# A two-stage attention model on one core: the first stage's Newton passes recompute their differences on TensorE

## The chip, the core and the metric

The kernel runs on one core of one Trainium2 chip. The metric is the device time of one execution in microseconds (us): the median of the kernel before is 6143.65 us over three runs (6131.52 to 6153.98).

## What is computed

Eight sequences of 512 tokens and 128 features go through one attention layer with a root-finding normalisation instead of a softmax, and then through six layers of windowed attention with a gated feed-forward block. Only the first layer, with the layer norms around it, is touched by the change:

```python
s = jnp.einsum('bhnd,bhmd->bhnm', Q, K) * scale            # 16 heads of 8 features
lam = jnp.where(mask, s, -1e30).max(-1) + 1.0              # causal mask
for _ in range(4):
    d = jnp.maximum(lam[..., None] - s, EPS)
    f = jnp.where(mask, 1 / d, 0.0).sum(-1) - 1.0
    fp = -jnp.where(mask, 1 / d ** 2, 0.0).sum(-1)
    lam = lam - f / fp
p = jnp.where(mask, 1 / jnp.maximum(lam[..., None] - s, EPS), 0.0)
return jnp.einsum('bhnm,bhmd->bhnd', p / p.sum(-1, keepdims=True), V)
```

So each head needs one row maximum, four Newton passes with two row sums each, and a final pass whose weights are multiplied with the values.

## The kernel before

Three stages run one after another: `stage1` (the first attention layer), `stage2` (the six layers) and `stage3` (a last transpose and sum). Each engine has its own written-out program, and semaphores order them.

In `stage1` the work is tiled as sequence, then quad (four heads; four quads), then head, then block of 128 query tokens. Because of the causal mask, query block u of a head needs 128·(u+1) keys, so a head has four units of 128, 256, 384 and 512 columns, 1280 columns in all, with the 128 queries on the partitions. The loop over sequences (`Fori(0, BATCH)`) holds four quads N, and while quad N is iterated, the scores of quad N+1 are made and the weights of quad N-1 are applied to the values.

- TensorE: `scores` (L212) multiplies 8 rows of queries with 8 rows of keys for each unit, once per quad, and adds the causal mask with an identity matmul (L214). The four heads of a quad sit on partitions 0, 32, 64 and 96, so each score matmul uses one group of 32 rows. `turn` (L225) transposes the finished weights, `weigh` (L238) multiplies them with the values (20 records for a head), `project` (L205) makes queries and keys.
- VectorE: `scores_in` (L489) copies scores into `S` with a running maximum; `newton` squares the root for even heads (L506, with the sum of 1/d) and squares again (L517, with the sum of 1/d²), then three tiny operations (L523, L525, L528) update `lam`.
- ScalarE: L386 makes 1/sqrt(lam - s) for each unit with `lam` as its bias, in five passes; L394 squares the odd heads; L358 copies transposed weights out of PSUM; L336 and L340 copy projections.
- GpSimd: L447 squares the final root into the weights `W`.

A matmul on fp32 data appears in the trace as two records, each with its own weight load. The lines at which the order is set on ScalarE are these:

```python
for t in range(ITERS + 1):
    for pair in (0, 1):
        if t:
            act.wait_ge(s_lam, N * 2 * ITERS + 2 * (t - 1) + pair + 1)
...
                nc.scalar.activation(R[:, h, c], S[:, par, h, c], ACT.Abs_reciprocal_sqrt,
                                     bias=lam[:, par, i:i + 1], scale=-1.0).then_inc(s_root, 1)
```

Of the kernel before, what the change touches and what calls it, by code (L numbers as in the profile page):

```python
# [18 lines left out]
P = 128  # L19
# [3 lines left out]
MASKED1 = -1e28  # L23
# [8 lines left out]
OFF = [sum(UNIT[:u]) for u in range(NBLK)]  # L32
# [3 lines left out]

ACT_SQ = [(t, h) for t in range(ITERS) for pair in (0, 1) for h in (2 * pair, 2 * pair + 1)
          if h % 2 == 1]
DVE_SQ = [(t, h) for t in range(ITERS) for pair in (0, 1) for h in (2 * pair, 2 * pair + 1)
          if (t, h) not in ACT_SQ]  # L40

PIECES = [(0, 3), (OFF[2], 3), (OFF[3], 4)]
BLOCKS = [[(0, 0), (1, 0), (1, 1)], [(2, k) for k in range(3)], [(3, k) for k in range(4)]]
NPC = len(PIECES)

# [16 lines left out]
NCONST = C_RO + 4 * SEQ  # L62


def stage1(nc, x, consts, w1qk, w1vo, x1d, hist):
    with ExitStack() as ctx:
# [10 lines left out]
        cmask = sb("cmask", [P, P])  # L77
        identb = sb("identb", [P, P], BF16)
        cmaskb = sb("cmaskb", [P, P], BF16)
# [12 lines left out]
        S = sb("S", [P, 2, QUAD, ROW])  # L92
        R = sb("R", [P, QUAD, ROW])
        W = sb("W", [P, QUAD, ROW])
        WT = sb("WT", [P, 2, SEQ])
# [3 lines left out]
        smax = sb("smax", [P, 2, NU])  # L99
        lam = sb("lam", [P, 2, NU])  # L100
        sum1 = sb("sum1", [P, NU])
        sum2 = sb("sum2", [P, NU])
        step = sb("step", [P, 2, NU])
        stat = [sb(f"stat{i}", [P, NBLK, 6]) for i in range(2)]
# [4 lines left out]
        psS = ps("psS", [P, NBLK, SEQ])  # L109
        psT = ps("psT", [P, 2, SEQ])  # L110
# [10 lines left out]
        s_score = sem("s_score")  # L121
        s_evac = sem("s_evac")
        s_lam0 = sem("s_lam0")
        s_root = sem("s_root")
        s_asq = sem("s_asq")
        s_dsq = sem("s_dsq")
        s_sq2 = sem("s_sq2")
        s_step = sem("s_step")
        s_lam = sem("s_lam")
        s_w = sem("s_w")  # L130
        s_tr = sem("s_tr")
        s_trev = sem("s_trev")
        s_pv = sem("s_pv")
        s_quad = sem("s_quad")
# [6 lines left out]
        s_rs = [sem("s_rs_in"), sem("s_rs_out")]  # L141

        M_PRO, M_B = 9, 13
        E_PRO, E_B = 9, 12
# [3 lines left out]

        @block.sync
        def _(sp):  # L150
            sp.dma_start(ident[:, :], consts[:, C_ID:C_ID + P]).then_inc(const_in, 16)
            sp.dma_start(cmask[:, :], consts[:, C_CM:C_CM + P]).then_inc(const_in, 16)
            sp.dma_start(wqk[:, :, :, :], w1qk).then_inc(const_in, 16)
            sp.dma_start(wvo[:, :, :], w1vo).then_inc(const_in, 16)
            sp.dma_start(xin[:, :, :], x[0].rearrange("(k p) d -> p k d", p=P)).then_inc(xin_in, 16)

            def tokens(t, i):
                return t[bass.ds(i, 1)].rearrange("a (k p) d -> p (a k) d", p=P)

            def store(b):  # L160
                sp.wait_ge(s_x1, b + 1)
                sp.dma_start(tokens(x1d, b - 1), x1[:, :, :]).then_inc(x1_out, 16)
                sp.wait_ge(s_mev, b * E_B + E_PRO + 2)
                sp.dma_start(hist[bass.ds(b - 1, 1)].rearrange("a p n -> (a p) n"), houtT[:, :])\
                  .then_inc(hist_out, 16)

            def sequence(b, last=False):
                first = isinstance(b, int) and b == 0
                if not first:
                    sp.wait_ge(s_x1, b)  # L170
                    sp.dma_start(xres[:, :, :], tokens(x, b - 1)).then_inc(xres_in, 16)
                sp.wait_ge(s_ln[0], b * LN + LN)
                if last:
                    sp.sem_inc(xin_in, 16)
                else:
                    sp.dma_start(xin[:, :, :], tokens(x, b + 1)).then_inc(xin_in, 16)
                if not first:
                    store(b)

            sequence(0)  # L180
            with sp.Fori(1, BATCH - 1) as b:
                sequence(b)
            sequence(BATCH - 1, last=True)
            sp.wait_ge(s_x1, BATCH)
            sp.dma_start(xres[:, :, :], tokens(x, BATCH - 1)).then_inc(xres_in, 16)
            store(BATCH)

            sp.wait_ge(x1_out, 16 * BATCH + 32)
            sp.wait_ge(hist_out, 16 * BATCH + 32)

        @block.tensor
        def _(pe):
            def m_free(n_ev):
                pe.wait_ge(s_mev, n_ev)

            def turn_h(base):
                pe.wait_ge(s_ln[0], base[1])
                m_free(base[0])
# [7 lines left out]

            def scores(N, j, h):


                for u in range(NBLK):  # L210
                    pe.wait_ge(s_evac, N * NU + h * NBLK + u + 1)
                    pe.matmul(psS[:, u, 0:UNIT[u]], qT[32 * h:32 * h + DH1, j, u * P:(u + 1) * P],  # L212
                              kT[32 * h:32 * h + DH1, j, 0:UNIT[u]], start=True, stop=True)
                    pe.matmul(psS[:, u, u * P:UNIT[u]], identb[:, :], cmaskb[:, :],  # L214
                              start=False, stop=True, skip_group_check=True).then_inc(s_score, 1)

            def turn(N, h, i):

                t = N * QUAD * NPC + h * NPC + i
                if i == 0:  # L220
                    pe.wait_ge(s_w, N * QUAD + h + 1)
                pe.wait_ge(s_trev, t + 1)
                c, n = PIECES[i]
                for m in range(n):
                    mm = pe.transpose(psT[:, (h * NPC + i) % 2, m * P:(m + 1) * P],  # L225
                                      W[:, h, c + m * P:c + (m + 1) * P], ident[:, :])
                mm.then_inc(s_tr, 1)

            def weigh(N, jprev, h, i):

                t = N * QUAD * NPC + h * NPC + i
                pe.wait_ge(s_trev, t + 3)
                if h == 0 and i == 0:
                    pe.wait_ge(s_attn, N + 1)
                for m, (u, k) in enumerate(BLOCKS[i]):
                    head = jprev * QUAD + h
                    o = (u * QUAD + h) * VW
                    mm = pe.matmul(psO[:, o:o + VW], WT[:, (h * NPC + i) % 2, m * P:(m + 1) * P],  # L238
                                   vals[:, k, head, :], start=(k == 0), stop=(k == u))
                mm.then_inc(s_pv, 1)  # L240

            def head_out(N, jprev, h):
                for i in range(NPC):
                    turn(N, h, i)
                    if i:
                        weigh(N, jprev, h, i - 1)
                weigh(N, jprev, h, NPC - 1)

            def turn_attn(b):
                pe.wait_ge(s_attn, b * NQ + 2)  # L250
                m_free(b * E_B + E_PRO)
# [4 lines left out]
            def out_project(b):  # L256
                m_free(b * E_B + E_PRO + 1)
# [5 lines left out]
            def turn_out(b):  # L263
                pe.wait_ge(s_ln[1], b * LN + LN)
                for k in range(NBLK):
# [3 lines left out]
            def values(b):  # L269
                m_free(b * E_B + E_PRO + 2)  # L270
                for k in range(NBLK):
                    mm = pe.matmul(psM[:, k * P:(k + 1) * P], hT[:, k * P:(k + 1) * P], wvo[:, 0, :],
                                   start=True, stop=True)
                mm.then_inc(s_m, 1)

            pe.wait_ge(const_in, 64)
# [6 lines left out]
            for j in range(NQ):  # L283
                project(0, j, 1 + 2 * j)
                project(1, j, 2 + 2 * j)
            pe.wait_ge(s_mev, E_PRO)
            for h in range(QUAD):
                scores(0, 0, h)

            with pe.Fori(0, BATCH) as b:  # L290
                for j in range(NQ):
                    N = b * NQ + j
                    nxt, prev = (j + 1) % NQ, (j - 1) % NQ
                    e = b * E_B + E_PRO
                    scores(N + 1, nxt, 0)
                    if j == 1:
                        pe.wait_ge(s_mev, e + 3)
                    head_out(N, prev, 0)
                    head_out(N, prev, 1)
                    scores(N + 1, nxt, 1)  # L300
                    head_out(N, prev, 2)
                    head_out(N, prev, 3)
                    scores(N + 1, nxt, 2)
                    if j == 0:
                        turn_attn(b)
# [1439 lines left out]
```

## Time and profile before

| what | value |
|---|---|
| median of three runs | 6143.65 us (6131.52 to 6153.98) |
| profiled execution, time / span | 6155.39 us / 6153.6 us |
| `stage1`: last store issued at (us from the span's start) | 2689.42 us |
| `stage2`: first DMA issued at / first matmul at | 2691.90 / 2705.69 us |
| one sequence in `stage1`, from the repetition of the trace | 327 us |

The profile is that of one execution. "Busy" is the time in which an engine executed at least one instruction; PEld is TensorE's loading of weights, which can overlap its matmuls. [...]

### The profile page before, as it was taken

To read this page: it belongs to the slowest core of one execution; us is meant where nothing else is said; L and a number is where in the kernel's file an instruction comes from. 1 tells how busy PE (TensorE), PEld (TensorE's weight loads), DVE (VectorE), ACT (ScalarE), POOL (GpSimd) and SP (SyncE) were. 2 spreads that over 40 slices of the span, in tenths; PEclk is the share of its full clock that TensorE was granted. 3 is DMA by queue.
4 is the path that set the end of the run, shared out by engine and by line. 5 is a ranking of instruction groups with operands and counts; after the bars stand their busy time and mean duration, and the time that the engine had idled before them with its cause. 6 is when DMAs were issued, how large, how long until landed. Compare 5 with 4: busy or idle time off the path is not lost. (4 is left out here: it accounts for less than half of the span.)

```text
span 6153.6 us, 167056 instructions
## 1 busy us (share of the span) xinstructions
PE 5086.1 (83%) x61548; PEld 2941.8 (48%) x61548; DVE 4768.3 (77%) x11291; ACT 3546.7 (58%) x6859; POOL 2569.4 (42%) x1151
## 2 busy tenths in 40 slices
PE   6777767676767776769999998999899999989996
PEld 3444444444444444435555554555455545545553
DVE  5777777777777777848888887888788888878884
ACT  4777776777767776745545554455454545444552
POOL 1101011111101011136666676667666667666672
PEclk9999999999999999999999999999999999999997
DMA  0000000000000000024445444444444444444443
GB/s 11 3 3 6 1 8 1 6 3 6 3 6 3 6 0 6 1 67 103 103 109 122 108 101 105 109 115 106 108 105 103 116 114 104 100 106 115 110 108 84
DMA packets 231561, 383.60 MB, mean 62 GB/s; under 512 B 35712, under 2 KB 60928, under 8 KB 230656
## 3 DMA queue, kind: packets, MB, share of 16 engines
q1 hardware_dynamic: 226560, 370.71, 25.6%
q8 instruction: 540, 8.85, 0.6%
q10 hardware_dynamic: 4224, 2.10, 0.1%
q14 instruction: 237, 1.94, 0.1%
HBM read 51.81 MB, written 18.87 MB: 11 GB/s over the span
## 5 line engine op out<-in xcount | busy, mean ns | idle before, releaser
L386 ACT ACTIVATE R<-S,lam 128x128 f32<-128x128 f32 (+3 forms) x2560 | 1191.1, 551 | 200.6 <-DVE lam L528 158.3
L447 POOL TENSOR_TENSOR W<-R 128x1280 f32<-128x1280 f32 x128 | 309.9, 2441 | 2335.6 <-ACT R L386 2335.6
L212 PE MATMUL psS<-kT,qT 8*128 8x128 f32 (+3 forms) x1056 | 755.3, 816 | 311.5 <-DVE S L489 222.2
L517 DVE CUSTOM_DVE_ANT_0 R<-R 128x128 f32<-128x128 f32 (+3 forms) x2048 | 987.1, 536 | 14.1
L1300 POOL TENSOR_TENSOR m<-m 128x1024 f32<-128x1024 f32 x384 | 902.5, 2361 | 69.7 <-DVE m L1408 69.4
L506 DVE CUSTOM_DVE_ANT_0 R<-R 128x128 f32<-128x128 f32 (+3 forms) x1024 | 503.3, 523 | 495.5 <-ACT R L386 471.3
L917 PE MATMUL pb<-xs,wg 128*128 128x512 f32 x1536 | 763.4, 632 | 49.8 <-DMA xs<-hist 36.5
L238 PE MATMUL psO<-vals,WT 128*128 128x9 f32 x2640 | 587.0, 356 | 160.8 <-ACT WT L358 160.8
L238 PEld LDWEIGHTS psO<-vals,WT 128*128 128x128 f32 x2640 | 589.4, 331 | 209.5 <-ACT WT L358 209.5
L1431 DVE SCALAR_TENSOR_TENSOR nf<-rn,m 128x1024 f32<-128x1024 f32 x384 | 617.0, 1638 | 87.5 <-ACT rn L1162 74.7
L1153 ACT ACTIVATE lnn<-pb,cst 128x1024 f32<-128x1024 f32 x192 | 213.9, 1114 | 803.0 <-PE pb L924 803.0
L1148 ACT ACTIVATE sq<-pb 128x1024 f32<-128x1024 f32 x384 | 382.0, 1021 | 490.7 <-PE pb L917 490.7
L1306 POOL TENSOR_TENSOR sm<-sm,mx 128x1024 f32<-128x1024 f32 x192 | 451.7, 2352 | 503.9 <-DVE mx L1422 503.8
L1296 POOL TENSOR_TENSOR sqs<-sq 128x1024 f32<-128x1024 f32 x192 | 457.0, 2380 | 225.6 <-ACT sq L1148 225.6
L1311 POOL TENSOR_TENSOR pr<-pr,rsum 128x1024 f32<-128x1024 f32 x192 | 410.8, 2140 | 289.1 <-DVE rsum L1444 285.2
L1407 DVE TENSOR_TENSOR m<-pb,tab 128x1024 f32<-128x1024 f32 x384 | 464.7, 1210 | 15.1 <-ACT sq L1148 12.1
L1408 DVE TENSOR_TENSOR m<-pb,tab 128x1024 f32<-128x1024 f32 x384 | 465.6, 1212 | 0.0
L394 ACT ACTIVATE R<-R 128x128 f32<-128x128 f32 (+3 forms) x1024 | 464.5, 458 | 0.0
L917 PEld LDWEIGHTS pb<-xs,wg 128*128 128x128 f32 x1536 | 291.1, 200 | 361.2 <-issue 354.0
L358 ACT COPY WT<-psT 128x384 f32<-128x384 f32 (+1 forms) x396 | 194.6, 509 | 461.9 <-PE psT L225 461.9
L212 PEld LDWEIGHTS psS<-kT,qT 8*128 8x128 f32 x1056 | 262.4, 307 | 407.7 <-DVE S L489 243.3
L924 PE MATMUL pb<-sqs,ones 128*128 128x512 f32 x768 | 392.5, 635 | 29.6 <-DVE m L1408 22.6
(112 smaller groups left out, 8709.3 us busy)
## 6 DMA issues: line engine op xcount, KB each, us to landing
qkn<-nf SPq DMA_DIRECT2D x1536, 128.0 KB
vr<-v SPq DMA_DIRECT2D x96, 768.0 KB, 6.0
vr<-v SPq DMA_DIRECT2D x96, 192.0 KB, 5.6
xr<-hist SPq DMA_DIRECT2D x48, 256.0 KB, 2.9
hist<-xo SPq DMA_DIRECT2D x48, 256.0 KB, 4.1
wg<-wqkv SPq DMA_DIRECT2D x24, 384.0 KB, 3.6
xs<-hist SPq DMA_DIRECT2D x48, 128.0 KB
vr<-v SPq DMA_DIRECT2D x96, 64.0 KB, 6.2
```

The costliest lines, as they stand in the source:

```text
L212: pe.matmul(psS[:, u, 0:UNIT[u]], qT[32 * h:32 * h + DH1, j, u * P:(u + 1) * P], kT[32 * h:32 * h + DH1, j, 0:UNIT[u]], start=True, stop=True)
L238: mm = pe.matmul(psO[:, o:o + VW], WT[:, (h * NPC + i) % 2, m * P:(m + 1) * P], vals[:, k, head, :], start=(k == 0), stop=(k == u))
L386: nc.scalar.activation(R[:, h, c], S[:, par, h, c], ACT.Abs_reciprocal_sqrt, bias=lam[:, par, i:i + 1], scale=-1.0).then_inc(s_root, 1)
L394: nc.scalar.activation(R[:, h, c], R[:, h, c], ACT.Square, accum_out=sum1[:, i:i + 1]).then_inc(s_asq, 1)
L506: nc.vector.tensor_tensor_reduce(out=R[:, h, c], in0=R[:, h, c], in1=R[:, h, c], scale=1.0, scalar=0.0, op0=ALU.mult, op1=ALU.add, accum_o ...
L517: nc.vector.tensor_tensor_reduce(out=R[:, h, c], in0=R[:, h, c], in1=R[:, h, c], scale=1.0, scalar=0.0, op0=ALU.mult, op1=ALU.add, accum_o ...
L917: mm = pe.matmul(out[:, half, :], wg[:, g, c:c + P], xs[:, 0:SEQ], start=True, stop=True)
L1296: nc.gpsimd.tensor_tensor(sqs[:, :, :], sq[:, :, 0, :], sq[:, :, 1, :], ALU.add).then_inc(s_sqs, 1)
L1300: nc.gpsimd.tensor_tensor(m1[:, which, :, :], m1[:, which, :, :], m2[:, which, ::-1, :], ALU.add)\
L1407: nc.vector.tensor_tensor(m1[:, which, :, :], src[:, :, :], tab[:, which, 0, :, :], ALU.mult)
L1408: nc.vector.tensor_tensor(m2[:, which, :, :], src[:, :, :], tab[:, which, 1, :, :], ALU.mult)\
L1431: nc.vector.scalar_tensor_tensor(out=nf[:, which, :, :], in0=rn[:, which, :].unsqueeze(1).broadcast_to([P, 2, SEQ]), scalar=1e12, in1=m1[: ...
```

## The change

`stage1` is rewritten; `stage2` and `stage3` stay. What is different:

- **Nine rows.** `lam` is put as a ninth row under the eight query rows, and a row of ones (`C_KR`) under the keys, whose evacuation multiplies by -SCALE1. So one matmul gives lam - s, and it is repeated for every pass: one pass for the minimum (p = 0), four Newton passes, one final pass (p = 5). `S` and the evacuation of scores go.
- **Pairs of heads.** `differences` issues the matmuls of two heads alternately, each head into its own three PSUM banks `psD[i]`, and then six bf16 mask matmuls. There is no second buffer: head i of the next pair waits until ScalarE has read head i of this one (`free`).
- **Whole heads.** ScalarE does one root of 128x1280 straight from PSUM and one square of 128x1280 for each head. VectorE takes the sums with four `bn_stats` of the square, from whose counts, means and variances eight small operations (`small`) make the new `lam`, for a whole quad.
- **lam's way back.** `lam` is transposed on VectorE and four DMAs put it into the ninth rows of `qT`.
- **The final pass** is made with keys and queries exchanged, so that the weights come out transposed; the transposes and their copies go.
- **Four quads in flight.** A table of 24 slots for each sequence, `SLOTS`, gives each slot one quad and pass: quad j does pass p in slot (5j + 4p) mod 24. Between two passes of one quad lie three other slots.

```diff
+NSLOT = 24
+LAST = ITERS + 1
+SLOTS = {}
+for _j in range(NQ):
+    for _p in range(LAST + 1):
+        SLOTS[(5 * _j + 4 * _p) % NSLOT] = (_j, _p, (5 * _j + 4 * _p) // NSLOT)
...
+            def send_lam(b, s):
+                j = SLOTS[s][0]
+                sp.wait_ge(s_lam, rank(b, s, UPDATE) + 1)
+                sp.sem_inc(held["sp"], 1)
+                for q in range(4):
+                    sp.dma_start(qT[DH1:P:32, j, :].rearrange("h (u q p) -> h u q p", u=NBLK, q=4)[:, :, q, :],
+                                 lamT[32 * q:32 * q + NU, j, :]).then_inc(lam_in[j], 16)
...
+                    if SLOTS[t[1]][1] == 0:
+                        pe.wait_ge(s_min, QUAD * rank(*t, FIRST) + h + 1)
+                    elif SLOTS[t[1]][1] == LAST:
+                        pe.wait_ge(s_rootf, QUAD * rank(*t, FINAL) + h + 1)
+                    else:
+                        pe.wait_ge(s_root, QUAD * rank(*t, NEWTON) + h + 1)
+                    pe.sem_inc(held["pe"], 1)
+
+                if p < LAST:
+                    for u in UORD:
+                        for i, h in enumerate(heads):
+                            if u == UORD[0]:
+                                free(i)
+                            r = slice(32 * h, 32 * h + KROW)
+                            pe.matmul(psD[i][:, UOFF[u]:UOFF[u] + UNIT[u]], qT[r, j, u * P:(u + 1) * P], kT[r, j, 0:UNIT[u]],
+                                      start=(u != UORD[2]), stop=True, skip_group_check=True)
...
+                for i, h in enumerate(heads):
+                    for c, n in spans:
+                        mm = pe.matmul(psD[i][:, c:c + n * P], identb[:, :],
+                                       cmaskb[:, int(p == LAST), 0:n, :].rearrange("p a n -> p (a n)"),
+                                       start=False, stop=True, skip_group_check=True)
+                    mm.then_inc(s_d, 1)
...
+                    act.wait_ge(s_d, QUAD * rank(b, s, range(LAST + 1)) + h + 1)
+                    nc.scalar.activation(dst, psD[i][:, 0:ROW], ACT.Abs_reciprocal_sqrt, bias=zero[:, 0:1])\
+                        .then_inc(s_rootf if p == LAST else s_root, 1)
...
+                    act.wait_ge(s_root, QUAD * rank(b, s, NEWTON) + h + 1)
+                    nc.scalar.activation(W[:, h, :], W[:, h, :], ACT.Square).then_inc(s_w, 1)
...
+                ins = nc.vector.bn_stats(out=stats[:, s % 2, i, :], in_=W[:, h, UOFF[u]:UOFF[u] + UNIT[u]])
```

On TensorE, at the head of the loop over sequences, the program before has one head's four units, each followed by its mask, once for a quad (`psS` are the scores in PSUM, `cmaskb` and `identb` mask and identity in bf16):

```order
L212 MATMUL psS<-kT,qT 128x128
L214 MATMUL psS<-cmaskb,identb 128x128
L211 REGISTER_ALU
L212 MATMUL psS<-kT,qT 128x256
L214 MATMUL psS<-cmaskb,identb 128x128
L211 REGISTER_ALU
L212 MATMUL psS<-kT,qT 128x384
L214 MATMUL psS<-cmaskb,identb 128x128
L211 REGISTER_ALU
L212 MATMUL psS<-kT,qT 128x512
L214 MATMUL psS<-cmaskb,identb 128x128
```

At the same place the changed program has this for a pair of heads (`x2` are the two heads; the two rows of 128x512 at the start stand apart, because each waits for its own bank):

```order
L298 ISA
L307 MATMUL psD<-kT,qT 128x512
L298 REGISTER_ALU
L307 MATMUL psD<-kT,qT 128x512
L307 MATMUL psD<-kT,qT 128x384 x2
L307 MATMUL psD<-kT,qT 128x128 x2
L307 MATMUL psD<-kT,qT 128x256 x2
L321 MATMUL psD<-cmaskb,identb 128x128
L321 MATMUL psD<-cmaskb,identb 128x256
L321 MATMUL psD<-cmaskb,identb 128x128 x2
L321 MATMUL psD<-cmaskb,identb 128x256
L321 MATMUL psD<-cmaskb,identb 128x128
```

Such a block now stands 48 times in the loop's body for each sequence, twice in each of 24 slots, where the scores of 16 single heads stood before.

On ScalarE, inside a pass, the program before works unit by unit (`R` is the root, `S` the scores in SBUF):

```order
L386 ACTIVATE R<-S,lam 128x128
L386 ACTIVATE R<-S,lam 128x256
L386 ACTIVATE R<-S,lam 128x384
L386 ACTIVATE R<-S,lam 128x512
L393 ISA
L394 ACTIVATE R,sum<-R 128x128
L393 REGISTER_ALU
L394 ACTIVATE R,sum<-R 128x256
```

The changed program has, for a pair of heads in a Newton slot, two roots out of PSUM and two squares, and then what else the slot holds:

```order
L469 ACTIVATE W<-psD,zero 128x1280
L465 REGISTER_ALU
L468 REGISTER_ALU
L469 ACTIVATE W<-psD,zero 128x1280
L479 ACTIVATE W<-W 128x1280 x2
L431 REGISTER_ALU
L432 COPY qT<-psM 128x512
```

Eight roots for two heads have become two, and they read the PSUM banks that TensorE has to fill again next.

## Rows read from the trace of the kernel before

**Rows 1.** The page: span, busy time of each engine.

```profile
span 6153.6 us, 167056 instructions
PE 5086.1 (83%) x61548; PEld 2941.8 (48%) x61548; DVE 4768.3 (77%) x11291; ACT 3546.7 (58%) x6859; POOL 2569.4 (42%) x1151
```

**Rows 2.** Busy time by stretch: a sequence of stage1, pieces of stage2.

```profile
core 0: us, PE busy (x) PEld busy (x) DVE busy (x) ACT busy (x) POOL busy (x), PEclk, DMA share, GB/s
350.00:677.00 327.00, 229.79 (x719) 146.70 (x718) 247.63 (x1046) 234.75 (x643) 38.74 (x16) 1.00 0.01 4
...
2731.68:2732.11 0.43, 0.43 (x33) 0.43 (x33) 0.00 (x0) 0.32 (x1) 0.43 (x1) 0.50 0.00 0
...
3300.00:6000.00 2700.00, 2546.06 (x44739) 1382.76 (x44737) 2237.07 (x2312) 1351.15 (x1398) 1815.49 (x814) 0.98 0.47 109
```

**Rows 3.** Waits between 350 and 677 us: us in total, times, longest.

```profile
DVE R L506 <- ACT R L386: 63.3, 17, 7.9
...
ACT R L386 <- DVE lam L528: 19.8, 4, 6.1
```

**Rows 4.** Timeline of TensorE, one head's scores in the prologue.

```profile
42.07 0.79 PE L212 MATMUL psS<-kT,qT 8*128 8x128 f32 x2
42.79 0.29 PE L214 MATMUL psS<-cmaskb,identb 128*128 128x128 bf16 x1
43.01 1.22 PE L212 MATMUL psS<-kT,qT 8*128 8x256 f32 x2
...
44.37 1.64 PE L212 MATMUL psS<-kT,qT 8*128 8x384 f32 x2
...
46.17 2.07 PE L212 MATMUL psS<-kT,qT 8*128 8x512 f32 x2
...
48.39 0.79 PE L212 MATMUL psS<-kT,qT 8*128 8x128 f32 x2
```

**Rows 5.** Timeline of TensorE where stage2 begins.

```profile
2705.69 5.92 PE L917 MATMUL pb<-xs,wg 128*128 128x512 f32 x8 [16.98 <-DMA xs<-hist]
2711.45 1.88 PE L989 MATMUL pb<-wg,xs 128*128 128x512 f32 x4
```

**Rows 6.** Timeline of TensorE: matmuls on eight tiles of 64 rows by 32 columns.

```profile
2728.00 3.75 PE L924 MATMUL pb<-sqs,ones 128*128 128x512 f32 x4 [2.94 <-POOL sqs L1296]
2731.68 2.06 PE L940 MATMUL pb<-qkn 64*32 64x64 f32 x128
```

**Rows 7.** Timeline of TensorE in stage1: values.

```profile
404.25 3.00 PE L238 MATMUL psO<-vals,WT 128*128 128x9 f32 x14
```

**Rows 8.** Groups by form, 340 to 667 us: busy us, mean ns of one.

```profile
L386 ACT ACTIVATE R<-S,lam 128x512 f32<-128x512 f32 x81 | 57.5, 710 | 0.0
L386 ACT ACTIVATE R<-S,lam 128x384 f32<-128x384 f32 x82 | 49.4, 603 | 0.0
L447 POOL TENSOR_TENSOR W<-R 128x1280 f32<-128x1280 f32 x16 | 38.7, 2442 | 285.8 <-ACT R L386 285.8
L205 PE MATMUL psM<-hT,wqk 128*128 128x512 f32 x16 | 16.4, 1130 | 13.2 <-ACT qT L336 11.2 <-ACT kT L336 2.0
L489 DVE TENSOR_SCALAR_CACHE_REDUCE S<-psS 128x512 f32<-128x512 f32 x16 | 11.0, 685 | 0.0
L525 DVE SCALAR_TENSOR_TENSOR step<-sum,step 128x8 f32<-128x8 f32 x32 | 7.5, 233 | 1.1
L489 DVE TENSOR_SCALAR_CACHE_REDUCE S<-psS 128x128 f32<-128x128 f32 x16 | 4.6, 290 | 0.0
L455 DVE BATCH_NORM_STATS2 stat<-x 128x6 f32<-128x128 f32 x4 | 0.9, 280 | 0.0
```

**Rows 9.** The page's groups: a square of 128x1024 out of PSUM.

```profile
L1148 ACT ACTIVATE sq<-pb 128x1024 f32<-128x1024 f32 x384 | 382.0, 1021 | 490.7 <-PE pb L917 490.7
```

**Rows 10.** DMA issues up to 2700 us: median us to landing.

```profile
x1d<-x SPq DMA_DIRECT2D x8, 256.0 KB, 2.3
```

**Rows 11.** Timeline of SyncE where stage1 ends.

```profile
2689.42 0.34 SPq L164 DMA_DIRECT2D hist<-houtT  x1
```

More of the change, by code:

```diff
@@ L35 @@
 VW = DH1 + 1
[L37 to L44, printed above, removed]
 DEPTH, H2, DH2, WIN = 6, 16, 64, 32
@@ L62 @@
 NCONST = C_RO + 4 * SEQ
+C_CT = NCONST
+C_KR = C_CT + P
+C_HC = C_KR + 1
+NCOLS = C_HC + 2 * NU
+UORD = (3, 2, 0, 1)
+UOFF = {u: sum(UNIT[w] for w in UORD[:i]) for i, u in enumerate(UORD)}
+KORD = (0, 3, 1, 2)
+KLEN = [SEQ - k * P for k in range(NBLK)]
+KOFF = {k: sum(KLEN[w] for w in KORD[:i]) for i, k in enumerate(KORD)}
+BANKS1 = 3
+KROW = DH1 + 1
+NSLOT = 24
[4 more added lines that the diff above has]
+        SLOTS[(5 * _j + 4 * _p) % NSLOT] = (_j, _p, (5 * _j + 4 * _p) // NSLOT)
 def stage1(nc, x, consts, w1qk, w1vo, x1d, hist):
@@ L107, in stage1 @@
         zero = sb("zero", [P, 1])
-        psS = ps("psS", [P, NBLK, SEQ])
-        psT = ps("psT", [P, 2, SEQ])
+        psD = [ps(f"psD{i}", [P, BANKS1 * SEQ]) for i in range(2)]
         psO = ps("psO", [P, SEQ])
@@ new lines, in rank, with fits, junk @@
+        def rank(b, s, passes, quad=None):
+            def fits(t):
+                return SLOTS[t][1] in passes and (quad is None or SLOTS[t][0] == quad)
+            if isinstance(b, int) and b == 0:
+                return sum(fits(t) for t in range(NSLOT) if t < s or not live(b, t))
+            return b * sum(fits(t) for t in range(NSLOT)) + sum(fits(t) for t in range(s) if live(b, t))
+        def junk(passes, quad=None):
+            return sum(SLOTS[t][1] in passes and (quad is None or SLOTS[t][0] == quad) for t in range(NSLOT) if SLOTS[t][2])
@@ L161, in store, with store_x1 @@
+            def store_x1(b):
                 sp.wait_ge(s_x1, b + 1)
+                sp.sem_inc(held["sp"], 1)
                 sp.dma_start(tokens(x1d, b - 1), x1[:, :, :]).then_inc(x1_out, 16)
[L163 to L167, printed above, removed]
-                first = isinstance(b, int) and b == 0
[L169 to L178, printed above, removed]
@@ L180, in _, with store_h @@
-            sequence(0)
-            with sp.Fori(1, BATCH - 1) as b:
[L182 to L186, printed above, removed]
+            def store_h(b, n_ev):
+                sp.wait_ge(s_mev, n_ev)
+                sp.sem_inc(held["sp"], 1)
+                sp.dma_start(hist[bass.ds(b - 1, 1)].rearrange("a p n -> (a p) n"), houtT[:, :]).then_inc(hist_out, 16)
@@ new lines, in body @@
+            def body(b):
+                first = isinstance(b, int) and b == 0
+                tail = isinstance(b, int) and b == BATCH
+                for s in range(NSLOT):
+                    if s == 0 and not first:
+                        sp.wait_ge(s_x1, b)
+                        sp.sem_inc(held["sp"], 1)
+                        sp.dma_start(xres[:, :, :], tokens(x, b - 1)).then_inc(xres_in, 16)
+                    if s == 1 and not tail:
+                        sp.wait_ge(s_ln[0], b * LN + LN)
+                        sp.sem_inc(held["sp"], 1)
+                        if isinstance(b, int) and b == BATCH - 1:
+                            sp.sem_inc(xin_in, 16)
+                        else:
+                            sp.dma_start(xin[:, :, :], tokens(x, b + 1)).then_inc(xin_in, 16)
+                    if s == 20 and not first:
+                        store_x1(b)
+                    if s == 23 and not first:
+                        store_h(b, b * E_B + E_PRO + (2 if tail else 9))
+                    t = prev(b, s)
+                    if live(b, s) and t is not None and SLOTS[t[1]][1] < LAST:
+                        send_lam(*t)
@@ L194, in m_free, with project, turn_h @@
                 pe.wait_ge(s_mev, n_ev)
-            def turn_h(base):
-                pe.wait_ge(s_ln[0], base[1])
-                m_free(base[0])
+                pe.sem_inc(held["pe"], 1)
+            def project(which, j, n_ev):
+                m_free(n_ev)
+                pe.matmul(psM[:, :], wqk[:, which, j, :], hT[:, :], start=True, stop=True).then_inc(s_m, 1)
+            def turn_h(n_ev, n_ln):
+                pe.wait_ge(s_ln[0], n_ln)
+                pe.sem_inc(held["pe"], 1)
+                m_free(n_ev)
                 for k in range(NBLK):
@@ L201, in turn_h @@
                 mm.then_inc(s_m, 1)
-            def project(which, j, n_ev):
-                m_free(n_ev)
-                pe.matmul(psM[:, :], wqk[:, which, j, :], hT[:, :], start=True, stop=True).then_inc(s_m, 1)
[L207 to L240, printed above, removed]
@@ new lines, in weigh @@
+            def weigh(b, s, h):
+                j = SLOTS[s][0]
+                r = rank(b, s, FINAL)
+                if h == 0:
+                    pe.wait_ge(s_attn, r + 1)
+                    pe.sem_inc(held["pe"], 1)
+                pe.wait_ge(s_wf, QUAD * r + h + 1)
+                pe.sem_inc(held["pe"], 1)
+                for u in range(NBLK):
+                    o = (u * QUAD + h) * VW
+                    for k in range(u + 1):
+                        c = KOFF[k] + (u - k) * P
+                        mm = pe.matmul(psO[:, o:o + VW], WF[:, h, c:c + P], vals[:, k, j * QUAD + h, :],
+                                       start=(k == 0), stop=(k == u))
+                mm.then_inc(s_pv, 1)
@@ L252, in turn_attn, with values @@
+            def values(n_ev):
+                m_free(n_ev)
+                for k in range(NBLK):
+                    mm = pe.matmul(psM[:, k * P:(k + 1) * P], hT[:, k * P:(k + 1) * P], wvo[:, 0, :], start=True, stop=True)
+                mm.then_inc(s_m, 1)
+            def turn_attn(b, n_ev):
+                pe.wait_ge(s_attn, rank(b, 12, FINAL) + 1)
+                pe.sem_inc(held["pe"], 1)
+                m_free(n_ev)
                 for k in range(NBLK):
@@ L267, in turn_out, with body @@
                 mm.then_inc(s_m, 1)
[L269 to L276, printed above, removed]
+            def body(b):
+                e = b * E_B + E_PRO
+                tail = isinstance(b, int) and b == BATCH
+                first = isinstance(b, int) and b == 0
+                for s in range(NSLOT):
+                    for pair in range(2):
+                        if live(b, s):
+                            differences(b, s, pair)
+                        for f in (1, 6, 11, 20):
+                            if s == f + 1 + pair and live(b, f):
+                                weigh(b, f, 2 * pair)
+                                weigh(b, f, 2 * pair + 1)
+                        if not tail:
+                            if (s, pair) == (2, 0):
+                                project(0, 1, e)
+                            if (s, pair) == (2, 1):
+                                project(1, 1, e + 1)
+                            if (s, pair) == (7, 0):
+                                project(0, 2, e + 2)
+                            if (s, pair) == (7, 1):
+                                project(1, 2, e + 3)
+                            if (s, pair) == (12, 0):
+                                project(0, 3, e + 4)
+                            if (s, pair) == (12, 1):
+                                project(1, 3, e + 5)
+                            if (s, pair) == (14, 0):
+                                values(e + 6)
+                        if (s, pair) == (15, 1):
+                            turn_attn(b, e + (0 if tail else 7))
+                        if (s, pair) == (16, 1):
+                            out_project(e + (1 if tail else 8))
+                        if (s, pair) == (20, 0):
+                            turn_out(b)
+                        if not tail:
+                            if (s, pair) == (21, 0):
+                                turn_h(e + 9, b * LN + 2 * LN)
+                            if (s, pair) == (22, 0):
+                                project(0, 0, e + 10)
+                            if (s, pair) == (22, 1):
+                                project(1, 0, e + 11)
@@ L419, in _ @@
-            for h in range(QUAD):
-                pieces(BATCH * NQ, h)
-            m = BATCH * M_B + M_PRO
-            evac(attnT[:, :], m + 1)
-            rstd(1, BATCH * LN + 3)
-            evac_out(BATCH)
+            evac(qT[:, 0, :], 2)
+            evac_keys(0, 3)
+            body(0)
+            with act.Fori(1, BATCH) as b:
+                body(b)
+            body(BATCH)
         @block.gpsimd
         def _(pool):
-            nc.gpsimd.memset(W[:, :, :], 1.0)
             nc.gpsimd.memset(vals[:, :, :, :], 1.0)
@@ L553, in _ @@
+            ins.then_inc(masks, 1)
             dve.wait_ge(masks, 2)
```

503 lines of the change are left out of this document (273 added, 230 removed).

## Prediction

> **What bounds the kernel now.** I read the page first [rows 1]: no engine is near 100% over the span, but the span is an average over two long stages. The busy time by stretch parts them [rows 2]: one sequence of `stage1` takes 327 us, in which VectorE is busy for 247.6, ScalarE for 234.8, TensorE for 229.8 and GpSimd for 38.7. Eight of these are 2616 us of the 2689 us at which the last store of the stage is issued [rows 11]; `stage2` isn't touched. The waits [rows 3] show what holds `stage1`: VectorE waits 63.3 us for ScalarE's root and ScalarE 19.8 us for VectorE's `lam`. They form one loop, root, square, sum, `lam`, and neither can run ahead. TensorE has about 100 us to spare in each sequence. The change takes work off this loop and puts it on TensorE, so the question is what a pair of heads costs there.
>
> **TensorE's clock in stage1.** The printed clock is no help here, because the first record of it comes later. The durations tell. A record of a projection, 128x512 on all 128 rows, takes 1130 ns [rows 8]; at the start of `stage2` four records of the same size take 1.88 us together, 0.43 us apart, where the eight before them took 5.92 [rows 5]. [...] In the prologue the four heads' scores follow one another as densely as they can (6.32 us for a head, from 42.07 to 48.39, the next starting at once), and the last still costs what the first did [rows 4]. Score matmuls on 8 rows don't raise the clock, even without a gap.
>
> **The new cycle.** A pair of heads now goes through a loop that has no second buffer: TensorE fills two sets of banks, ScalarE reads them, TensorE fills them again. [...]
>
> - *Score stream of one head.* From 384 to 512 columns the duration grows from 1.64 to 2.07 us, 0.43 us for 128 columns, so 1280 columns stream in 4.3 us; each matmul has 0.36 us beside that (0.79 - 0.43) [rows 4]. Nine rows instead of eight use the same group of 32 and cost the same.
> - *Do the two heads overlap?* The trace has no pair of such matmuls, but it has others: 128 records on eight tiles, two row groups by four column groups, take 2.06 us [rows 6], at a granted clock of 0.50 [rows 2]. At that clock 128 columns stream in 0.43 us over two records, so a record of 64 columns takes 0.107, and 128 of them in a line 13.7 us. They ran 6.6 deep; column groups alone give at most four, so both row groups worked at once. I take full overlap: the pair streams in 4.3 us, counted from the later head.
> - *Masks.* One mask takes 0.21 us from its start to the next instruction (42.79 to 43.01) [rows 4]. The pair has six, with eight blocks of 128 columns: between 0.8 us (half of 0.21 for each block, if the weight load hides) and 1.7; I take 1.3, of which head A's end comes 0.4 earlier.
> - *Roots.* A unit of 512 takes 710 ns and one of 384 takes 603, so 0.84 ns for a column [rows 8]; 1280 columns give 1.35 us. A square of 1024 columns from PSUM takes 1021 ns [rows 9], by which 1280 would be 1.24. I take 1.3 for a root and 1.25 for a square.
>
> Count from the moment at which head A's masks have landed: root A until 1.3, root B until 2.6, with 0.1 for the semaphore head B's stream runs from 2.7 to 7.0 (head A's, begun 1.3 earlier, is hidden behind it), and head A's masks land 0.85 later: **7.85 us for a pair**. The squares (2 x 1.25) run meanwhile. Bounds: with roots of 1.24 and masks of 0.8 in all, 7.45; with the 0.36 of four matmuls unhidden, 9.3.
>
> **The sum for one sequence.** 24 slots of two pairs, 48 x 7.85 = 377 us (in the four slots of the first pass VectorE's minimum of 1280 columns, (685-290)/384 = 1.03 ns for a column [rows 8], stands in for the root, 1.4 us and some small operations between: +4). The values: 14 records take 3.00 us [rows 7], 0.214 each; 20 records for a head, 40 for a pair, are 8.6 us, of which the next pair's wait for root A hides 1.3: 8 pairs x 7.3 = 58. The projections (two records of about 1 us [rows 8]), the output projection and the transposes each lie in the same gap and stick out by about 0.7 us: +10. Together **449 us against 327**, +122, and eight times that +976. At the ends: the first sequence has no other quad to fill slots 1 to 3, the last one's chain of passes runs nearly alone, and there is a tail as before; about +15 in all. That is +991 on the profiled 6155, so 7146, and as the median lies 12 us below that execution, **7135 us**.
>
> **What is hidden, and by what.** ScalarE has 80 roots and 64 squares, 184 us, and some 7 for copies: 191 of 449. VectorE: `bn_stats` of 128 columns takes 0.22 us from one to the next (0.9 us for four) [rows 8], so a head takes 4 x 0.22 + 768 x 1.03 ns = 1.7 us, 64 heads 107 us; 16 minima 22; 20 updates of eight operations at 0.23 [rows 8], 37; norms some 13: 179. GpSimd stays at 38.7. `lam`'s way back is about 2 us of small operations, four issues and a landing of about 2.3 us [rows 10], against three slots of 15.7 us before it is needed. SyncE's queue has it behind the stores of `x1` and `hist`, whose data are ready slots earlier. If that cover went, the stall would be TensorE's, at the first matmul of a slot, with everything queued behind.
>
> [...]
>
> **The rivals.**
>
> 1. *The clock rises in stage1: faster.* TensorE's activity grows (two row groups at once, masks on 128 rows, a projection right behind them). [...] For: `stage2` holds the high clock over 2700 us [rows 2]. Against: rows 4, and that TensorE must stop for each root. [...] Chance 0.14.
> 2. *The row groups don't overlap: slower still.* Each record waits for the one before, as within one head in rows 4. Head B's stream then starts when A's ends: 1.4 + 8.6 = 10.0 instead of 7.0, +3.0 us, and 384 x 3.0 = 1150: **about 8290 us**. For: every fp32 matmul is two records with weight loads on the same group, issued head by head. Against: rows 6. With partial overlap it lies between. Chance 0.12.
> 3. *The change doesn't bind on TensorE at all* but on another term that I hide (the small operations, the DMA of `lam`, code loading): each slot would then be longer by a few us without a busier engine, 7300 to 8000 us. Chance 0.05. That the time stays within 0.3% needs a cycle of 6.1 us by accident; 0.01.
>
> The forecast has 0.68. Its own range follows from 7.45 and 9.3 us: 384 x (-0.4) and 384 x 1.45 give 6980 to 7690. With the second and third rival the range is **6900 to 8300**, which leaves out the faster case and the extremes. A measurement of this kernel tells about 0.3% from no change: faster 0.15, same 0.02, slower 0.83.
>
> **What the changed kernel's profile would show.** Right: a sequence of about 450 us; L307 records of 128x512 at about 1.06 us or longer, two heads' records overlapping in time; TensorE idle some 1.4 us before each pair, released by ScalarE's root; ScalarE busy for about 40% of `stage1`, VectorE too; almost no wait for `lam`. Wrong: L307 records of 128x512 near 0.6 us (rival 1); a pair's masks 10 us after its first matmul (rival 2); waits for the DMA of `lam` (rival 3).

## The result, and the profile after

| | time | against before |
|---|---|---|
| before, runs beside it | 6148.81 us (6131.52 to 6169.75, 4 runs) | |
| changed kernel | 7011.18 us (6984.98 to 7029.06, 4 runs) | ratio 1.1397 [1.1346, 1.1449] |

The change costs 862 us; 986 (7135 - 6149) were forecast. The page of the changed kernel, beside [rows 1], has the span, the engines' busy time and the granted clock in 40 slices:

```profile
span 6983.2 us, 169488 instructions
PE 6343.6 (91%) x67000; PEld 3832.7 (55%) x67000; DVE 4023.9 (58%) x6681; ACT 3143.1 (45%) x3001; POOL 2545.1 (36%) x1151
...
PE   7899998989989899898969999989989998998996
...
PEclk6555555555555555555579999999999999999998
```

Against the kernel before VectorE lost 744 us of work and ScalarE 404, and TensorE gained 1258. The clock line now has records for `stage1`, where [rows 2] prints 1.00 for a stretch without one: 0.5 for most of it. Here the low clock is the 0.50 of such lines and the high clock their 1.00. Two stretches, with the columns of [rows 2]:

```profile
1000.00:1500.00 500.00, 453.12 (x1647) 302.40 (x1646) 183.43 (x562) 209.49 (x183) 36.76 (x16) 0.52 0.01 3
...
4000.00:6900.00 2900.00, 2723.40 (x48316) 1482.81 (x48315) 2401.34 (x2496) 1448.67 (x1498) 1945.31 (x874) 0.98 0.47 109
```

In `stage1` TensorE is busy for 91% of the time, VectorE for 37% and ScalarE for 42%; `stage2` looks as before. The waits between 1000 and 2000 us, beside [rows 3] (who waits, for whom, us in total, times, longest):

```profile
DVE stats L605 <- ACT W L479: 569.9, 76, 22.9
ACT W L469 <- PE psD L321: 292.3, 69, 9.1
...
PE psD L307 <- ACT W L469: 46.7, 42, 1.3
...
PE psD L307 <- DVE part L598: 22.7, 21, 3.6
```

VectorE waits for ScalarE's squares, ScalarE for TensorE's masks, and TensorE for nothing but ScalarE's (or, in the first pass, VectorE's) reading of the banks, 1.1 us on average. No wait for `lam`'s DMA is on the list. So the loop without a second buffer should be what bounds `stage1`; the experiments below test it. The timeline shows two turns of it:

```profile
1010.66 2.02 PE L265 MATMUL psM<-hT,wqk 128*128 128x512 f32 x2
...
1012.61 3.01 PE L307 MATMUL psD<-kT,qT 9*128 9x512 f32 x16
...
1015.55 0.61 PE L321 MATMUL psD<-cmaskb,identb 128*128 128x128 bf16 x6
...
1017.45 5.82 PE L307 MATMUL psD<-kT,qT 9*128 9x512 f32 x16 [1.29 <-ACT W L469]
...
1023.21 1.03 PE L321 MATMUL psD<-cmaskb,identb 128*128 128x128 bf16 x6
1023.85 2.55 ACT L469 ACTIVATE W<-psD,zero 128x1280 f32<-128x1280 f32 x2 [3.01 <-PE psD L321]
1023.89 2.23 SPq L212 DMA_DIRECT2D qT<-lamT  x4
...
1024.03 8.65 PE L338 MATMUL psO<-vals,WF 128*128 128x9 f32 x40
```

The pair at 1017.45 is the usual one: 16 records for both heads in 5.82 us, where one head took 6.32 with its masks in [rows 4]. The pair at 1012.61 ran mostly at the high clock, right behind masks and a projection: 3.01 us. Its true counterpart is not the usual pair but the pair at the same place one sequence earlier. That one stands behind a projection too, has no wait for a root in its stream, and ran at the low clock (the last three rows are stretches around the pair at 1012.61, with the columns of [rows 2]; the clock stands before the last two numbers):

```profile
570.78 5.16 PE L307 MATMUL psD<-kT,qT 9*128 9x512 f32 x16
575.87 1.03 PE L321 MATMUL psD<-cmaskb,identb 128*128 128x128 bf16 x6
...
1010.50:1013.20 2.70, 2.70 (x7) 1.11 (x5) 0.00 (x0) 2.70 (x3) 0.00 (x0) 0.50 0.00 0
1013.30:1016.60 3.30, 2.86 (x22) 2.04 (x20) 2.39 (x6) 3.23 (x4) 0.00 (x0) 1.00 0.00 0
1016.80:1023.00 6.20, 5.55 (x16) 3.66 (x16) 3.94 (x16) 4.04 (x4) 0.00 (x0) 0.50 0.01 3
```

So the high clock makes 3.0 us of 5.2. There were 23 such spells in the whole of `stage1`, together 79 us of 3556. The queue issues the four DMAs of `lam` within 2.23 us; the profile gives no time at which they land. Groups by form, 1000 to 1440 us:

```profile
L307 PE MATMUL psD<-kT,qT 9*128 9x512 f32 x160 | 117.7, 1094 | 33.0 <-ACT W L469 18.8 <-DVE part L598 9.8 <-ACT WF L469 4.3
...
L469 ACT ACTIVATE W<-psD,zero 128x1280 f32<-128x1280 f32 x64 | 81.5, 1323 | 124.5 <-PE psD L321 124.2
L479 ACT ACTIVATE W<-W 128x1280 f32<-128x1280 f32 x64 | 77.6, 1266 | 0.0
...
L598 DVE TENSOR_REDUCE part<-psD 128x10 f32<-128x1280 f32 x16 | 23.4, 1486 | 21.1 <-PE psD L321 18.4 <-issue 2.8
```

### The profile page after: what moved, and what is told of

It is laid out like the page before. It is cut to its first block and busy times, and to the rows that moved or that the text cites. A ratio compares the mean times of both kernels' runs of the same rounds, so it can differ in the third digit from the quotient of the medians.

```text
span 6983.2 us, 169488 instructions
## 1 busy us (share of the span) xinstructions
PE 6343.6 (91%) x67000; PEld 3832.7 (55%) x67000; DVE 4023.9 (58%) x6681; ACT 3143.1 (45%) x3001; POOL 2545.1 (36%) x1151
## 5 line engine op out<-in xcount | busy, mean ns | idle before, releaser
L605 DVE BATCH_NORM_STATS2 stats<-W 128x6 f32<-128x512 f32 (+3 forms) x2048 | 882.1, 480 | 2011.6 <-ACT W L479 2011.6
L307 PE MATMUL psD<-kT,qT 9*128 9x128 f32 (+3 forms) x5120 | 1734.7, 734 | 267.2 <-ACT W L469 151.2
L307 PEld LDWEIGHTS psD<-kT,qT 9*128 9x128 f32 x5120 | 1047.9, 313 | 907.9 <-issue 883.9
L552 POOL TENSOR_TENSOR WF<-WF 128x1280 f32<-128x1280 f32 x128 | 294.1, 2319 | 3219.9 <-ACT WF L469 3219.9
L469 ACT ACTIVATE W<-psD,zero 128x1280 f32<-128x1280 f32 x512 | 651.7, 1323 | 1013.7 <-PE psD L321 1011.9
L479 ACT ACTIVATE W<-W 128x1280 f32<-128x1280 f32 x512 | 620.7, 1266 | 0.0
L338 PEld LDWEIGHTS psO<-vals,WF 128*128 128x128 f32 x2560 | 550.2, 331 | 3.5
L338 PE MATMUL psO<-vals,WF 128*128 128x9 f32 x2560 | 550.1, 360 | 0.0
L469 ACT ACTIVATE WF<-psD,zero 128x1280 f32<-128x1280 f32 x128 | 163.0, 1324 | 657.7 <-PE psD L321 657.7
L316 PE MATMUL psD<-qT,kT 9*128 9x512 f32 (+3 forms) x1024 | 374.0, 752 | 70.0 <-ACT WF L469 27.8
```

Of the source, the lines that this page charges most:

```text
L307: pe.matmul(psD[i][:, UOFF[u]:UOFF[u] + UNIT[u]], qT[r, j, u * P:(u + 1) * P], kT[r, j, 0:UNIT[u]], start=(u != UORD[2]), stop=True, skip_ ...
L338: mm = pe.matmul(psO[:, o:o + VW], WF[:, h, c:c + P], vals[:, k, j * QUAD + h, :], start=(k == 0), stop=(k == u))
L469: nc.scalar.activation(dst, psD[i][:, 0:ROW], ACT.Abs_reciprocal_sqrt, bias=zero[:, 0:1])\
L479: nc.scalar.activation(W[:, h, :], W[:, h, :], ACT.Square).then_inc(s_w, 1)
L605: ins = nc.vector.bn_stats(out=stats[:, s % 2, i, :], in_=W[:, h, UOFF[u]:UOFF[u] + UNIT[u]])
```

## The experiments

My theory: TensorE's stream at the low clock and the wait for the roots follow one another in a loop; two heads overlap almost fully. The rivals: no overlap, a clock that could be raised, or a bound elsewhere.

### The two heads one after the other

```diff
-                    for u in UORD:
-                        for i, h in enumerate(heads):
+                    for i, h in enumerate(heads):
+                        for u in UORD:
```

(and the same for `KORD` in the final pass)

> The changed kernel, but differences issues all four matmuls of head A and then all four of head B instead of alternating; same work, same masks, same waits. My theory (the two row groups stream at once, and this hides one head's 4.3 us in each cycle of 7.87): without alternation head B's stream starts when head A's ends, the cycle grows by about 3 us to 10.9, a sequence by 48 x 3 = 145 us, and the time is about 7011 + 1150 = 8160 us. Rival (the overlap comes from the queue, whatever the order of issue, or the cycle is bound elsewhere): the cycle stays near 7.9 and the time within 100 us of 7011.

Measured: 7766.78 us (one run, as are the next four), between the 8160 of the theory and the 7011 of its rival. Its timeline of TensorE:

```profile
1029.43 7.75 PE L307 MATMUL psD<-kT,qT 9*128 9x512 f32 x16 [1.08 <-ACT W L469]
1037.11 1.03 PE L321 MATMUL psD<-cmaskb,identb 128*128 128x128 bf16 x6
1039.23 7.75 PE L307 MATMUL psD<-kT,qT 9*128 9x512 f32 x16 [1.08 <-ACT W L469]
```

The pair's stream grows from 5.82 to 7.75 us and the cycle, from one pair's first record to the next one's, from 7.87 to 9.80 (1029.43 to 1039.23): the alternation is worth 1.93 us for each pair, so the heads do overlap in the changed kernel, and rival 2 is out. But without any overlap head B would start 4.40 us behind head A (one head's stream, below) instead of 1.22, so 3.2 us were to be expected, and I had expected about 3. The records say why it is less. In a window of 20 ns, 1032.54 to 1032.56, three of them are at work (count, shortest/median/longest duration in ns, first and last start, forms):

```profile
L307 PE MATMUL psD<-kT,qT x3: 416/842/1217, 1031.9 to 1032.5; 9*128 9x384 f32 x1, 9*128 9x128 f32 x1, 9*128 9x512 f32 x1
```

Head A's order is 512, 384, 128, 256 columns, two records each. Head B's first record of 512 is at work here while only one of A's last four has started, though the program issues it behind all of them. Head B overtakes: it starts 3.12 us behind head A, 1.27 of the two streams still overlap, and that was missing from my forecast.

### All 32 rows of a group

```diff
-                            r = slice(32 * h, 32 * h + KROW)
+                            r = slice(32 * h, 32 * h + 32)
```

> The changed kernel with 32 rows in each difference matmul instead of 9; rows 9 to 31 of queries and keys are zeros, so the results are the same. Theory (a matmul costs by its columns, and the row group is taken whole): records of 128x512 keep their 1.06 us between starts, the cycle stays 7.87, and the time is 7011 within 30 us. [...]

Measured: 6990.99 us, within the changed kernel's range. The median cycle is 7.87 us again, and the granted clock in 1000 to 3000 us stays near 0.5:

```profile
1000.00:3000.00 2000.00, 1806.46 (x6517) 1194.19 (x6517) 714.60 (x2177) 847.51 (x733) 165.46 (x72) 0.52 0.01 4
```

The time at the high clock in `stage1` is 154 us instead of 79, but the granted clock of the whole execution, 0.752, lies within the 0.734 to 0.755 of the changed kernel's four runs. Nine rows or 32 cost the same, as I had taken for eight and nine, and with 32 the clock of `stage1` is as low as with nine.

### Filler matmuls on 128 rows

```diff
+                    for n in range(FILL * (i == 0)):
+                        pe.matmul(psD[1][:, ROW:ROW + 2 * P], identb[:, :], cmaskb[:, 0, :, :].rearrange("p a n -> p (a n)"),
+                                  start=False, stop=True, skip_group_check=True)
```

They stand behind head A's masks, where head A's root runs beside them, and write columns that nobody reads. Four:

> The changed kernel with four more bf16 matmuls of 128 rows by 256 columns in each pair, between head A's masks and head B's, into the unused end of head B's banks. [...] Theory (the slow clock is what makes the new first stage slow, and what lifts it is full-height activity): the printed clock in the first stage rises well above 0.51, pairs at 5.7 to 6.1 us appear in number, and the time falls below 6800. Rival (this much doesn't lift the clock): the clock stays near 0.51 and the time near 7011, up to 7150 if the four are not hidden.

Eight:

> [...] If the clock stays slow, they stick out by about 0.8 us less what root A hides: cycle 7.9 to 8.7, time 7011 to 7320. If the clock rises for good, the cycle is 5.7 to 6.2 us and the sequence 48 x 6 + 30 = 320 us, and the time is near 6100, the kernel before.

Measured: 7088.79 us with four, 7073.73 with eight. Four give 85 us at the high clock in `stage1`, hardly more than the 79 without them, so what was called the rival came true. Eight give 597 us in 167 spells, which is neither of the two cases that I had named. The clock of the window and a turn of the loop with eight:

```profile
1000.00:2000.00 1000.00, 972.70 (x4113) 636.05 (x4114) 365.84 (x1091) 430.70 (x364) 78.18 (x34) 0.60 0.01 3
...
1030.86 1.91 PE L327 MATMUL psD<-cmaskb,identb 128*128 128x256 bf16 x8
...
1033.13 3.97 PE L308 MATMUL psD<-kT,qT 9*128 9x512 f32 x16
```

The pair's stream takes 3.97 us here, partly at the high clock, and the fillers 1.9. The cycles (from masks to masks) fall mainly into two groups, 8.8 us at the low clock and 6.6 with a spell in them. Against the 7.87 without fillers the first lose 0.9 (the 0.8 of the forecast was my estimate) and the second gain 1.3, and the total comes out 63 us longer. So eight fillers raised the clock in part, to 0.60 in this window, but not for a profit.

### Half a root

```diff
-                    nc.scalar.activation(dst, psD[i][:, 0:ROW], ...)
+                    nc.scalar.activation(dst[:, 0:ROW // 2], psD[i][:, 0:ROW // 2], ...)
```

(`W` and `WF` are filled with ones once, at the start.) This kernel leaves out the root of half the columns, so it tells about time only.

> The changed kernel with the root taken of only the first 640 of 1280 columns; the other half of W and WF keeps its initial ones, so the Newton sums are not the reference's. Theory (the pair's cycle is root A, root B, head B's stream and the masks, one after another, because the banks have no second set): a root takes about 0.8 us instead of 1.33, two of them are 1.1 us shorter from start to start, and the cycle falls from 7.87 to about 6.8; 40 of 48 pairs have a root, so 8 x 40 x 1.1 = 350 us less, 6660 us. Rival (TensorE itself is full, it only looks as if it waited): the cycle falls by less than 0.3 and the time by less than 100 us.

Measured: 6798.74 us. The root takes 790 ns instead of 1323, and two turns are

```profile
1035.92 5.29 PE L307 MATMUL psD<-kT,qT 9*128 9x512 f32 x16 [0.55 <-ACT W L469]
1041.14 1.03 PE L321 MATMUL psD<-cmaskb,identb 128*128 128x128 bf16 x6
1042.72 5.29 PE L307 MATMUL psD<-kT,qT 9*128 9x512 f32 x16 [0.55 <-ACT W L469]
```

6.80 us apart. Both roots are on the path: 1.07 us less of them takes 1.07 off the ordinary cycle, although only 0.53 of it shows as a shorter idle time (from 1.08 to 0.55). The other half is in the stream, which shrinks from 5.82 to 5.29, because head B's first record no longer waits as long behind head A's. The total lies above the 6660 forecast, for two reasons. A sequence takes 409.5 us, 27.5 less than the changed kernel's, where 40 times 1.1 was expected. Of its 48 pairs, 8 wait for minima instead of roots and 8 have 8.65 us of values over the roots, and neither give anything; 6 have a projection there and give 0.5 each; 26 give 1.07. That makes 31 us, of which the rarer high clock (48 us of `stage1` instead of 79) takes back some 3. And what follows the first matmul of `stage2` took 3459.7 us instead of 3427.4 in this execution.

### bf16 rows in three parts

Queries and keys in bf16, each as a near part and a remainder: a group of 32 rows holds three products of eight rows and `lam` in two rows, 26 in all. A bf16 matmul is one record instead of two, and in the changed kernel at the low clock a bf16 mask record of 256 columns is followed by the next 0.21 us later, an fp32 record of 256 columns 0.43 us later. VectorE makes the remainder as the projection is read, `lam` goes through eight DMAs, and the scale moves into the root.

```diff
-        qT = sb("qT", [P, NQ, SEQ])
-        kT = sb("kT", [P, NQ, SEQ])
+        qT = sb("qT", [P, NQ, SEQ], BF16)
+        kT = sb("kT", [P, NQ, SEQ], BF16)
...
+                nc.vector.scalar_tensor_tensor(out=(qT, kT)[which][:, j, :], in0=near[:, :], scalar=fixed[:, 1 + which:2 + which],
+                                               in1=psM[:, :], op0=ALU.mult, op1=ALU.add).then_inc(s_mev, 1)
...
+                nc.vector.tensor_tensor(lamb[:, j, 1, 0:NU], l, lamb[:, j, 0, 0:NU], ALU.subtract).then_inc(s_far, 1)
```

> [...] 40 pairs at 4.9 and 8 first ones at 5, values 8 x 7, others 10: about 305 us for a sequence against 324.5 in the kernel before, 8 x 305 + 45 + 3450 = 5935 us. Rival (the loop over TensorE and ScalarE has other costs that the stream covers, such as lam's DMAs or weight loads): the cycle stays above 6 us and the time above 6400.

Measured: 5928.02 us (5923.32 to 5931.36, 4 runs), ratio to before 0.9634 [0.9613, 0.9656]. The clock did not change (0.52 between 1000 and 2000 us), the stream did. Its timeline:

```profile
1047.88 1.22 PE L314 MATMUL psD<-kT,qT 26*128 26x512 bf16 x7 [0.82 <-DVE part L615]
...
1049.04 1.03 PE L328 MATMUL psD<-cmaskb,identb 128*128 128x128 bf16 x6
1049.68 2.55 ACT L480 ACTIVATE W<-psD,zero 128x1280 f32<-128x1280 f32 x2 [2.97 <-PE psD L328]
...
1052.12 2.43 ACT L490 ACTIVATE W<-W 128x1280 f32<-128x1280 f32 x2
...
1052.37 1.22 PE L314 MATMUL psD<-kT,qT 26*128 26x512 bf16 x7 [0.64 <-ACT W L480]
...
1053.53 1.03 PE L328 MATMUL psD<-cmaskb,identb 128*128 128x128 bf16 x6
...
1054.44 2.54 ACT L480 ACTIVATE W<-psD,zero 128x1280 f32<-128x1280 f32 x2
```

The masks stand 4.49 us apart (1049.04 to 1053.53) instead of 7.87. Roots and squares now fill ScalarE without a gap in this stretch, 4.76 us from root to root, which is also the median cycle (the 4.9 of the forecast was my estimate): in the pairs without values the bound has moved there. In the stage as a whole ScalarE is busy for 612 of 1000 us, and the pairs behind which the values stand take 10.6 to 12.5 us, in which ScalarE waits for TensorE. A sequence takes 301 us, under the 324.5 of before. With all else of the change in place, and a little work added on VectorE and the queue, a shorter stream turns 14% slower into 3.6% faster.

### The values over four slots

```diff
-                            if s == f + 1 + pair and live(b, f):
-                                weigh(b, f, 2 * pair)
-                                weigh(b, f, 2 * pair + 1)
+                            if s in (f + 1, f + 2) and live(b, f):
+                                weigh(b, f, 2 * (s - f - 1) + pair)
```

One head's 20 records now follow each pair, so that each block can hide behind a root, instead of 40 behind every other pair. On the changed kernel:

> The changed kernel with one head's product with the values behind each of four pairs, instead of two heads' behind each of two pairs of the same two slots. Theory (of each such block the next pair's wait for root A hides about 1.4 us, and the rest is on the path): four blocks hide 5.6 us where two hid 2.8, 4 x 2.8 = 11 us for a sequence, so the time falls by about 90 us to 6920. Rival (what sticks out isn't on the path, because ScalarE catches up later): no difference within 20 us.

Measured: 6964.81 us (6954.18 to 6979.29, 4 runs), ratio to before 1.1319 [1.1287, 1.1352]; the interval of the change itself begins at 1.1346. The two overlap, so the ratios alone don't show a gain, though all four times lie under the changed kernel's lowest, 6984.98. The trace shows it: a sequence takes 432 us, 5 less, where 11 were expected. The high clock fell from 23 spells to 3 (79 us to 10); 20 spells of 2.2 us are 5.5 us for a sequence, which is the half that is missing. On the bf16 rows:

> The two last edits together. With a cycle bound by ScalarE at 4.9 us, TensorE has a little time of its own in each cycle, so a block of 4.3 us sticks out by some 2.5 us instead of 7.2 for a double one: 16 x 2.5 = 40 against 57 us; about 288 us for a sequence and 5800 us. If the values aren't on the path any more, both edits together cost the same as the bf16 rows alone.

Measured: 5836.52 us (5826.56 to 5846.93, 4 runs), ratio to before 0.9494 [0.9471, 0.9516]. One sequence is 287 us, of which ScalarE works 182 and TensorE 210:

```profile
1800.00:2087.00 287.00, 209.94 (x1036) 134.73 (x1036) 174.33 (x518) 182.20 (x158) 36.59 (x16) 0.51 0.02 4
```

This is the fastest version, 5% under the kernel before; 288 us for a sequence and 5800 us were expected.

## Why the prediction held, point by point

- **What bounds.** Right. The path was to be root A, root B, head B's stream, head A's masks. Counted from the moment at which head A's masks have landed, the trace has head A's first record at 1.48 us, head B's at 2.70, the next masks at 7.23 and A's masks landed at 7.87. The forecast had 2.7, 7.0 and 7.85. The median of 384 cycles is 7.87 us. Two errors cancel in it: head B's stream and what follows it took 4.53 instead of 4.3, head A's masks 0.64 instead of 0.85. The test with half a root shows that both roots belong to the path, that with bf16 rows that the stream does.
- **Overlap.** Right, and shown by the records of the pair and by the heads in turn: taking the alternation away adds 1.93 us. Head B's stream, 4.40 us from its first record (1018.67) to the end of its last (1023.07 by its spacing), is as long as the 4.27 of one head's 1280 columns at the spacing of its records (0.427 for a record of 256 columns, 0.854 for 512) within 0.13. The chance of 0.12 for rival 2 was put on a case whose extreme did not occur even with the heads issued in turn: there they still overlap in part.
- **Clock.** Right for the most part: the terms of the cycle were those of a low clock, and `stage1` has 0.51 to 0.52, though TensorE is busy for 91% of it. The trace of before has no record of the clock in `stage1`; but at 0.50 the changed kernel's records of 256 columns follow one another at 0.427 us, the same rate as the 0.43 for 128 columns over two records of [rows 4]. Not foreseen were the 23 short spells. In 22 of them one cycle takes 5.7 us instead of 7.87, 2.2 less; with three of them a sequence is some 7 us shorter. The high clock is thus within reach of `stage1`, for moments, and rival 1 did deserve a chance. The 6.1 us of a cycle at which the time would stay the same was an estimate that no run shows; the runs have 437 us for a sequence with the median cycle at 7.87 and 301 us with it at 4.76, against 324.5 before.
- **The sum of a sequence.** 437.0 us instead of 449. By term: 48 x 7.867 = 377.6 (377 forecast); the minima +6 (4), at 9.04 and 8.21 us for the two pairs of a slot, because the reduction takes 1.49 us; the values +56.6 (58), between 6.1 and 8.0 us for a block; the spells -7 (0); and the rest +3.7 (10), all of it in two pairs. The projections, which I had sticking out by 0.7 us each, cost nothing: a pair behind one at the low clock has the same cycle of 7.87, because the projection fills the wait for the root. The sequence of before, read from a stretch as 327, is 324.5 by the distance from one sequence's projections to the next one's. So the difference is 112.5 instead of 122, and eight times that 900 instead of 976: 76 of the error.
- **The ends.** The wrong sign, 65 us off. Before, the end of `stage1` ([rows 11], 2689.4) exceeds eight periods by 93 us; after (3539.0) by 43. I had +15, and it is -50. The step that failed is that I counted only what the new ends add, an amount for which I had no row, and not what the old ones had. Some 15 us of it lie in the prologue: the kernel before made all eight projections first and began its scores at 35.75 us, the changed one begins its first differences at 21.19. Where the other 50 lie is open.
- **Stage 2.** From its first matmul on the changed kernel's profiled execution takes 3427 us, that of before 3448. Nothing in it was changed; the executions profiled here lie between 3427 and 3460, so these 20 us can't be put down to the change. The steps together: 991 - 76 - 65 - 20 = 830, the difference of the two spans.
- **What is hidden.** Right. VectorE has 183 us in 500, ScalarE 209, and no wait for the DMAs of `lam` is on the list. How long they take to land isn't shown.

What stays open: why the clock rose behind some masks and projections and not behind all, and what would keep it up. The fillers show only that eight for each pair reach it in part (597 us of `stage1` instead of 79) and cost more than they bring (63 us in the total). A second set of banks, which would take the roots out of the loop, was not tried.

## What to carry to other kernels

Work that is moved to an idle engine has to be priced in a cycle, not in busy time: TensorE had 100 us to spare in each sequence and got some 157 more (1258/8), which already is too much, and this loop with one set of banks adds the roots to its stream (roots 1.07 us shorter took 1.07 off the cycle). Where a recomputation on TensorE is to pay, price its stream first. In fp32 head B's stream was eight records in 4.53 us; with bf16 parts it was four in 1.16 at the same low clock, and the same design went from 14% slower to 3.6% faster, and with the values spread to 5%. And read a period from one point of the loop to the same point of the next turn, and subtract the old ends before adding the new ones.

## What the runs showed of the hardware

- **Records of two row groups started out of the program's order, in the two stretches looked at.** In the changed kernel head A's first record of 384 columns starts at 1019.290 and head B's second of 512 at 1019.656, though the program issues them the other way round. The records carry no head's name; which is whose follows from their lengths and their spacing. With the heads in turn head B's first record starts at 1032.549, when three of head A's (from 1032.756 on) are still to come. The records of one group keep their order in both stretches. With the heads in turn 1.27 us of the two streams thus overlap without any alternation.
- **The clock rose for 3.4 us at a time and fell again** in `stage1` of the changed kernel: 23 spells, 79 us in all; in 22 of them one pair's stream, behind masks and a projection, takes about 3.0 us instead of 5.2.
